# Eighteen filler products on TensorE ahead of the first transposes of an attention and FP4 feed-forward block

## The reference

```
x = x + attn(layernorm(x))          # attn has a layer norm of its own, with gamma and beta
    xn  = layernorm(.) * gamma + beta
    qkv = xn @ w_qkv                # 128 -> 3 * 16 heads * 64
    q, k = rotate(q), rotate(k)     # rotary embedding
    out = softmax(q k^T / 8) v
    out @ w_out + b_out
x = x + ffn(layernorm(x))
    fp4_linear(silu(fp4_linear(x, w_gate)) * fp4_linear(x, w_up), w_down)   # 128 -> 352 -> 128
```

## Time and profile before

| what | value |
|---|---|
| median of 3 runs | 1512.1 us (1511.99 to 1512.59) |
| profiled execution | 1511.85 us, span 1510.0 us |
| TensorE busy | 1437.1 us, 95% |
| VectorE busy | 1213.9 us, 80% |
| ScalarE busy | 919.0 us, 61% |
| GpSimd busy | 1347.2 us, 89% |
| mean granted TensorE clock | 0.985 |
| TensorE's first instruction | 14.73 us |

### The profile page before, as it was taken

How to read it: one execution, slowest core, us unless ns; L and a number is a source line. 1 busy time by engine, 2 the same in 40 slices (tenths; PEclk the granted TensorE clock), 3 DMA queues, 4 the chain that set the end, 5 groups by cost and what they waited for, 6 DMA issues and landing times.

```text
span 1510.0 us, 27777 instructions
## 1 busy us (share of the span) xinstructions
PE 1437.1 (95%) x10281; PEld 762.1 (50%) x10281; DVE 1213.9 (80%) x1632; ACT 919.0 (61%) x1398; POOL 1347.2 (89%) x789
## 2 busy tenths in 40 slices
PE   4799999999999999999999999999999999999686
PEld 2345555555554555555555455555555555554455
DVE  7888887777878888887788887878788888774886
ACT  2366666666666676666666666766666666664443
POOL 3599999989899999999889999999999999986695
PEclk9899999999999999999999999999999999999898
DMA  5211121121112111111111211212221111100001
GB/s 145 48 39 50 36 51 43 49 51 50 41 35 50 46 42 50 44 48 51 50 45 30 50 46 40 51 42 50 50 50 41 35 50 44 39 17 24 1 21 35
DMA packets 69206, 67.24 MB, mean 45 GB/s; under 512 B 26512, under 2 KB 52432, under 8 KB 69072
## 3 DMA queue, kind: packets, MB, share of 16 engines
q1 hardware_dynamic: 69072, 65.46, 17.2%
HBM read 29.25 MB, written 2.62 MB: 21 GB/s over the span
## 4 chain that ended last, share of the span: by engine, by line
PE 73%; POOL 14%; DVE 7%; issue 3%; ACT 2%; DMA 0%; POOLq 0%; SPq 0%; ACTq 0%; DVEq 0%
PE po L1261 24%; PE st L1248 20%; PE mx L1309 9%; PE ms L1289 7%; POOL psum_keys L412 7%; PE ms L1341 3%; PE ms L1274 3%; PE ms L1330 3%; POOL kq L550 1%; DVE negmax L933 1%; PE ms L1317 1%; POOL queries_lo L563 1%; PE st L1400 1%; POOL probs L433 1%; POOL probs L432 1%
## 5 line engine op out<-in xcount | busy, mean ns | idle before, releaser
L412 POOL TENSOR_TENSOR psum_keys<-psum_keys,probs 128x1024 f32<-128x1024 f32 x224 | 533.2, 2381 | 43.6 <-ACT probs L681 18.8
L681 ACT ACTIVATE probs<-st 128x1024 f32<-128x1024 f32 x512 | 497.6, 1028 | 120.7 <-PE st L1248 116.3
L1261 PE MATMUL po<-probs,v 128*64 128x512 f32 x2048 | 483.5, 593 | 0.0
L933 DVE TENSOR_REDUCE negmax<-mx 128x2 f32<-128x1024 f32 x322 | 393.1, 1221 | 96.2 <-PE mx L1309 95.7
L1261 PEld LDWEIGHTS po<-probs,v 128*64 128x64 f32 x2048 | 141.7, 137 | 219.0 <-issue 165.1
L935 DVE TENSOR_REDUCE negmax<-mx 128x1 f32<-128x512 f32 x186 | 128.4, 690 | 141.5 <-PE mx L1309 141.0
L1309 PE MATMUL mx<-keys_hi,queries_hi 64*128 64x512 f32 x1016 | 229.5, 448 | 12.3 <-DVE negmax L933 6.4
L1248 PE MATMUL st<-queries_hi,keys_lo 64*128 64x512 f32 x1024 | 202.2, 391 | 0.0
L1248 PE MATMUL st<-queries_lo,keys_hi 64*128 64x512 f32 x1024 | 201.8, 390 | 0.0
L1248 PE MATMUL st<-queries_hi,keys_hi 64*128 64x512 f32 x1024 | 201.4, 390 | 0.0
L1309 PEld LDWEIGHTS mx<-keys_hi,queries_hi 64*128 64x128 f32 x1016 | 95.8, 185 | 161.0 <-issue 98.5
(11 more groups left out here) (185 smaller groups left out, 1913.1 us busy)
## 6 DMA issues: line engine op xcount, KB each, us to landing
kq<-sin_part SPq DMA_DIRECT2D x256, 128.0 KB, 2.4
rsum<-recips SPq DMA_DIRECT2D x128, 128.0 KB, 2.9
wqkv<-in_L_attn_w_qkv_dram SPq DMA_DIRECT2D x32, 192.0 KB, 2.8
resid<-in_L_attn_x_dram SPq DMA_DIRECT2D x4, 512.0 KB, 7.8
wout<-in_L_attn_w_out_dram SPq DMA_DIRECT2D x32, 64.0 KB, 2.5
out_dram<-resid SPq DMA_DIRECT2D x8, 256.0 KB, 2.3
sums<-sums_kept SPq DMA_DIRECT2D x64, 4.0 KB
spread<-sums SPq DMA_DIRECT2D x64, 4.0 KB, 1.6
```

Source lines behind the costliest of these rows:

```text
L412: nc.gpsimd.tensor_tensor(psum_keys[:, c], first, probs[:, (STEPS * P + i) % RING], ALU.add)\
L681: nc.scalar.activation(probs[:, step_n % RING], st[step_n % 2][:, :], ACT.Exp, scale=SCALE)\
L933: nc.vector.tensor_reduce(out, banks[:, :], AX.X, ALU.max, negate=True).then_inc(mx_free, 1)
L1261: last = mm(po[HD * a:HD * a + HD, :], v[:, P % 2, KEY_ORDER[jt], HD * a:HD * a + HD], probs[:, step_n % RING, a], start=(jt == 0), stop=( ...
```

## The change

A function `fill(n)` is added to TensorE's program. It issues n fp32 products of `ones` (64 columns of weights) with the 256 columns of `maxcol` into 64 partitions of `ms`. `fill(18)` stands ahead of the transposes, behind the waits for `const_done` and `one_rows_done`. The wait for `ln_in` moves behind the fill. The result in `ms` is not used, and no semaphore is raised. No other engine's program changes.

```
-        pe.wait_ge(ln_in, 48)
+
+        def fill(n):
+
+            for _ in range(n):
+                mm(ms[0:HD, 0:2 * PART], ones[:, :], maxcol[:, :].rearrange("p c n -> p (c n)"), start=True, stop=True)
+
         pe.wait_ge(const_done, 1)
         pe.wait_ge(one_rows_done, 2)
+        fill(18)
+        pe.wait_ge(ln_in, 48)
         for c in range(2):
             pe.wait_ge(xn_done, HALF * c + HALF)
```

## The result

The changed kernel took 1513.54 us (median of 22 runs, 1510.83 to 1517.22), the kernel before 1511.9 us (22 runs, 1509.92 to 1513.06). The ratio is 1.0014, 95% interval 1.0008 to 1.002: 1.2 to 3.0 us slower, a small loss that stands clear of the noise, where the forecast was +0.45 us. Timed again with the experiments the ratio was 1.0011 (1.0002 to 1.002).

What follows compares the result with a forecast made beforehand. TensorE bounds the bulk, but VectorE's small operations and weight quantisation bound the start. Terms 0 + 0.45 + 0 on the 1512.1 us median gave 1512.6 us, no measurable change; range with rivals 1510.5 to 1514.9.

Steps and rivals of the forecast that it cites:

- The forecast's own range: Whole kernel's time if the forecast itself holds, without the rivals' ends: 1511.8 to 1513.4 us, chance 0.64.
- the forecast's own sign: Mechanism wrong if VectorE's 20.98 moves, V keeps 1.09, or the stage after 31 us changes by over 1 us.
- Start and end of the fill: Ahead of the transposes: fill starts at 3.57 us and ends at 12.8 to 14.4, before 14.73.
- One filler 0.85 or 0.43 us: In the fill: each filler takes 0.85 us at the low clock, 0.43 at the high.
- Nothing gained, VectorE is late next: First K and Q projections: TensorE finishes 2.2 us earlier, but VectorE still starts at 20.98; gain 0.
- V at the low clock, +0.45 us at the start: First V projection: 0.89 us longer after 5.3 us idle, less 0.44 spare on ScalarE; bounds 0 and +0.9.
- The spells after 31 us as before, nothing else anywhere: Low-clock spells after 31 us: expected unchanged, 0 with a spread of about 1 us.
- rival C: After 31 us: low-clock spells grow by another projection or two, +1.5 to +2.5 us, 1514.1; chance 0.14.
- Rival A: At the fill: clock not lifted, or too late, delaying the first units; 1514.8 to 1516.4 us, chance 0.10.
- Rival B: Between 27 and 55 us: some low-clock spells vanish, up to 3.3 us, put at 1.5; 1510.6, chance 0.12.

Runs made afterwards that it cites:

- the kernel with 28 instructions more: The change plus 7 fillers of 4 columns between the last K unit and the first V projection: 1512.19 us, ratio 1.0.
- the one with narrow fillers: The change with its 18 fillers cut from 256 columns to 4, the same 72 instructions: 1513.73 us, ratio 1.0015.
- the bridge: The change plus 11 fillers between the last K unit and the first V projection: 1512.89 us, ratio 1.0008.
- 68 and 72: Instructions added to the kernel before: 68 by gap fillers without first fill (ratio 0.9991), 72 by the change (1.0014) or 18 fillers of 4 columns (1.0015).
- the three kernels at 100 and 256: Kernels with 100 (two) or 256 (one) instructions more than the kernel before, by added or substituted 4-column fillers: 1512.19, 1512.5 and 1512.18 us.

## Why the prediction was right, and where it was short

The time lay in the range of 1510.5 to 1514.9, and the forecast of no change by 0.2% holds for the ratio 1.0014, though its interval reaches 1.002. That is partly luck. The forecast's own range ended at 1513.4 and the measured 1513.54 is just outside it; the +0.45 us is outside the measured 1.2 to 3.0; what held was the wider range, made wide for the rivals. And by the forecast's own sign its mechanism was wrong in one part: the stage after 31 us was to gain or lose no more than 1 us, and from the start of the rounding of the keys to the end of the span it lost 1.5 us in the first profile and 2.1 in the second. By its steps:

- *Start and end of the fill*: said 12.8 to 14.4; measured 3.66 to 14.06. Right. The pace turned near 8.6 us, 5.0 us after the start: in the windows of that line alone 2 or 3 products each half microsecond up to 8.5 us, then 4. In the second profile it turned a microsecond earlier.
- *One filler 0.85 or 0.43 us*: right. At these paces 5.0 us hold 12 of the 36 instructions and the other 24 take 5.2 us, 10.2 together; measured 10.40, and 9.84 in the second profile.
- *Nothing gained, VectorE is late next*: right. 20.82 with the change, 20.98 before, less the 0.15 us of the load.
- *V at the low clock, +0.45 us at the start*: measured +0.47 in one profile, +0.32 in the second. The size was right to 0.15 us. The rounding of the keys was said for 31.2 and started at 30.92, with the earlier load taken off 0.31 us late: ScalarE began it 0.11 us before the copy ahead of it ended, which the sum did not allow for. As the main cause of the measured loss it fell: the kernel with 28 instructions more pays it (start +0.67) and is level with before, and the one with narrow fillers doesn't pay it and is as slow as the change.
- *The spells after 31 us as before, nothing else anywhere*: this is the step that failed, with the words of rival C, "nothing after 31 us has new work". The sum put nothing there without a row that showed it, and lacked a term: the bulk's +0.92 and +1.18 us in the two profiles, by fetches of TensorE's instructions beside swaps that GpSimd waits for. The three times of before could not warn of it, since the fetches of their program fall on swaps with room to spare. Nor did their 0.6 us show the scatter: 22 runs of before spread over 3.1 us, the 22 of the change over 6.4.
- *Rival A*: not so; zeros in half the array lifted the clock. *Rival B*: not by the change. But its pool was sized well: 3.3 us was its limit, and keeping the clock high shortens the start by 2.8 us and the time by 2.9 (ratio 0.9981). *Rival C*: its number, 1514.1, came nearest to the measured time, but not its cause: in the second profile the spells behind V are as before, and the loss is there too.

V ran at the low clock in every kernel with the long fill and no fillers of full width between it and V, and at the high clock with the bridge. With that the trace agrees with the rule of the Trainium skill (TensorE: Matmul & The Clock Gate, HAM oscillation — how this bites in real kernels) that a wait behind a burst brings the clock down.

What stays open: by what means a fetch slows the issuing of transfers beside it (the view gives one packet, not its DMA engine); why one program fetched first at 48 us in one execution and at 40 in the next; and whether other offsets than 68 and 72 of the 256 are as bad.

## What to carry to other kernels

Ask of every instruction put in front of a long unrolled program what it does to the moments of the instruction fetches, and time the same number of idle instructions as a control: here 72 that do nothing cost as much as the change. Then move the program by some tens of idle instructions more: an offset at which the fetches meet covered transfers costs nothing. On this kernel a fill pays where something waits for TensorE's next product behind it, in the gaps after the projections, and not ahead of them. An engine that is not on the path, warmed early, only waits earlier.

## What the hardware showed that I had not expected

- A single fetch of 16 KB beside the issuing of four small transfers stretches it from at most 2.71 us to as much as 3.74. Where the engine behind them has no room, it waits up to 1.2 us more: 1.88 to 2.40 against 1.24 us in the bulk, 0.60 to 1.11 against none at 31 us.
- The 22 runs of the change scatter more than those of before, 1510.83 to 1517.22 against 1509.92 to 1513.06 us, and so do the 18 narrow fillers; the three kernels at 100 and 256 do not. The same program fetched first at 48 us in one execution and at 40 in another, so which swaps it meets can differ from run to run; that this makes the scatter is likely and not shown.
- The column of the granted clock showed 1.00 through the first 24 us in every profile, while fillers and projections ran at both paces; there only durations tell the level.
- Products of 4 columns cost 3.97 us for 36 at the start of the program, 0.11 us each with their weight load, and did not lift the clock. Padding with them costs time where TensorE has none to spare.
- V ran at the low clock after 2.29 us of idle time in one kernel and at the high one after 3.12 to 3.15 in three others: the idle time just before a product does not decide its clock by itself.
